# A decoder layer on one core: the eighth input of the first two feed-forward tiles last, and statistics ahead of the neighbour's finish

## The reference

```
h = silu(lin(x, w1)) * lin(x, w2)          # 256 -> 1024
h = gelu(lin(h, h1))                       # 1024 -> 1024
h = gelu(lin(h, h2))                       # 1024 -> 1024
y = lin(h, w3)                             # 1024 -> 256
x = layernorm(x + y)
```

## Time and profile before

| what | us |
|---|---|
| median of 3 runs | 927.42 |
| the profiled execution: its time | 932.09 |
| the profiled execution: its span in the trace | 930.3 |
| VectorE busy | 499.5 (54%) |
| ScalarE busy | 374.1 (40%) |
| GpSimd busy | 313.4 (34%) |
| mean granted clock of TensorE | 0.949 of full speed |

### The profile page before, as it was taken

The page is one execution under the profiler, slowest core; times in us unless marked ns, Lnnn a source line. Parts: engine busy times, 40 slices in busy tenths (PEclk is TensorE's granted clock), DMA queues, the critical chain, the costliest instruction groups (busy, mean ns, idle before and its releaser), DMA issues.

```text
span 930.3 us, 14113 instructions
## 1 busy us (share of the span) xinstructions
PE 865.7 (93%) x5066; PEld 572.7 (62%) x5066; DVE 499.5 (54%) x1299; ACT 374.1 (40%) x758; POOL 313.4 (34%) x553
## 2 busy tenths in 40 slices
PE   7779999898998999899999999999989999999996
PEld 5544444345766777786666644443467677887885
DVE  5597878625775432264444778873266752126113
ACT  0566666673444211232111366655635432123120
POOL 4403223136312544343132314213332143335333
PEclk9866989999999999999999889987799999999999
DMA  9800534240001233343231023520000000000000
GB/s 307 356 1 3 190 130 137 92 169 2 1 2 42 96 94 110 113 129 98 91 95 66 25 114 137 191 106 2 1 1 1 2 1 0 1 7 18 1 1 24
DMA packets 23894, 68.69 MB, mean 74 GB/s; under 512 B 4400, under 2 KB 11568, under 8 KB 23600
## 3 DMA queue, kind: packets, MB, share of 16 engines
q1 hardware_dynamic: 23824, 67.77, 20.8%
HBM read 65.40 MB, written 13.63 MB: 85 GB/s over the span
## 4 chain that ended last, share of the span: by engine, by line
PE 78%; DVE 13%; ACT 3%; issue 3%; POOL 2%; POOLq 0%; DVEq 0%; ACTq 0%
PE bank_pair L842 25%; PE bank_pair L667 7%; PE bank_pair L649 7%; PE bank_pair L618 7%; PE bank_pair L830 6%; DVE bank_pair L1165 4%; PE bank_pair L760 4%; DVE max_raw L1163 3%; PE bank_pair L699 3%; PE bank_pair L839 3%; PE bank_pair L604 3%; PE bank_pair L562 2%; PE bank_pair L772 2%; PE bank_pair L749 2%; PE bank_pair L716 1%
## 5 line engine op out<-in xcount | busy, mean ns | idle before, releaser
L986 ACT ACTIVATE prob_s<-bank_pair 128x512 f32<-128x512 f32 (+3 forms) x384 | 163.5, 495 | 86.7 <-PE bank_pair L649 85.8
L1455 POOL TENSOR_TENSOR hid_lo_s<-act_raw_s,hid_hi_s 128x512 fp32r<-128x512 f32 x96 | 124.3, 1295 | 216.8 <-DVE hid_hi_s L1321 176.5
L618 PE MATMUL bank_pair<-k_t_s,q_t_s 64*128 64x512 f32 (+3 forms) x384 | 149.2, 467 | 13.7 <-DVE max_raw L1165 7.6
L1165 DVE CUSTOM_DVE_ANT_0 bank_pair<-bank_pair,causal_bf 128x128 f32<-128x128 f32 (+3 forms) x256 | 123.4, 509 | 54.0 <-PE bank_pair L618 52.6
L1426 POOL TENSOR_SCALAR_AFFINE_SELECT prob_s<-prob_s 128x128 f32<-128x128 f32 x256 | 72.2, 297 | 170.0 <-ACT prob_s L986 166.8
L649 PE MATMUL bank_pair<-q_t_s,k_t_s 64*128 64x512 f32 (+3 forms) x384 | 119.0, 423 | 3.9 <-DVE resid_f_s L1285 1.7
L1321 DVE CAST hid_hi_s<-act_raw_s 128x512 fp32r<-128x512 f32 x64 | 31.7, 496 | 153.8 <-ACT act_raw_s L1047 153.8
L649 PEld LDWEIGHTS bank_pair<-q_t_s,k_t_s 64*128 64x128 f32 x384 | 60.3, 202 | 80.6 <-ACT prob_s L986 50.2
L618 PEld LDWEIGHTS bank_pair<-k_t_s,q_t_s 64*128 64x128 f32 x384 | 68.7, 207 | 62.9 <-issue 20.3
L1047 ACT ACTIVATE act_raw_s<-bank_pair,scales 128x512 f32<-128x512 f32 x64 | 43.7, 689 | 157.3 <-PE bank_pair L842 157.3
L1163 DVE TENSOR_REDUCE max_raw<-bank_pair 128x1 f32<-128x512 f32 x128 | 83.0, 685 | 43.1 <-PE bank_pair L618 43.1
(11 more groups left out here) (156 smaller groups left out, 1444.4 us busy)
## 6 DMA issues: line engine op xcount, KB each, us to landing
ring_s<-scratch SPq DMA_DIRECT2D x34, 512.0 KB, 3.3
home_s<-scratch SPq DMA_DIRECT2D x22, 512.0 KB, 5.9
checked_s<-in_w_ffn SPq DMA_DIRECT2D x2, 3584.0 KB, 17.8
scratch<-in_w_ffn SPq DMA_DIRECT2D x2, 2560.0 KB, 10.9
ring_moved_s<-scratch SPq DMA_DIRECT2D x10, 512.0 KB, 3.3
checked_s<-in_w_ffn SPq DMA_DIRECT2D x1, 4096.0 KB, 30.9
x_t_s<-in_x_t SPq DMA_DIRECT2D x2, 1024.0 KB, 5.2
x_tok_s<-in_x SPq DMA_DIRECT2D x2, 1024.0 KB, 8.7
```

The source lines that it names most:

```text
L618: mm(out[:, 0:k1 - k0], qkt(q, p, 0)[r, P * qt:P * (qt + 1)], qkt(q, p, 1)[r, k0:k1], start=True, stop=True).then_inc(S["max_mm"], 1)
L986: act.activation(prob[q][4 * (s % 2) + j][:, 0:n], S_BANK[j][:, 0:n], ACT.Exp, scale=SCALE).then_inc(S["exp_done"], 1)
L1165: dve.tensor_tensor_reduce(out=out[:, 0:left], in0=out[:, 0:left], in1=L["causal_bf"][:, CHUNK - left:CHUNK], scale=1.0, scalar=NEG, op0=A ...
L1455: pt(dst[1][:, m], act_raw[q][r % 3][:], dst[0][:, m].bitcast(F32), ALU.subtract).then_inc(S["f_lo"], 1)
```

## The change

The table of work is built by a new function. For h1, h2 and w3 the first two groups are written together: inputs 0 to 6 of tile 0, inputs 0 to 6 of tile 1, then input 7 of tile 0 and input 7 of tile 1. The groups from the third on are as before. On VectorE `out_finish` of a w3 tile is now issued behind `out_stats` of the next tile of its chunk, and that of the last tile (m = 3) one slot later at the end of `f_work`.

```diff
--- before.py
+++ after.py
@@ -214,13 +214,30 @@
     (1, 1, ("h2",), ("F", 1, 44), ("F", 1, 51)),
     (1, 1, ("w3",), ("F", 1, 52), ("F", 1, 55)),
 ]
+
+
+def products_in_order(groups):
+
+
+    last = KH - 1
+    work = []
+    for n, (layer, m) in groups:
+        if layer in ("w1", "w2"):
+            work += [(n, i) for i in range(4)]
+        elif m == 0:
+            work += [(n + j, i) for j in range(2) for i in range(2 * last)]
+            work += [(n + j, i) for j in range(2) for i in range(2 * last, 2 * KH)]
+        elif m >= 2:
+            work += [(n, i) for i in range(2 * KH)]
+    return work
+
+
 F_MM = [[] for _ in range(END_SLOT)]
 F_DONE = {}
 F_START = {}
 for _q, _c, _layers, _a, _b in PLAN:
     _a, _b = SLOT_AT[_a], SLOT_AT[_b]
-    _work = [(n, i) for n, (c, layer, m) in enumerate(GROUPS) if c == _c and layer in _layers
-             for i in range(4 if layer in ("w1", "w2") else 16)]
+    _work = products_in_order([(n, (layer, m)) for n, (c, layer, m) in enumerate(GROUPS) if c == _c and layer in _layers])
     for _j, (n, i) in enumerate(_work):
         _k = max(_a + _j * (_b - _a + 1) // len(_work), F_DONE.get((_q, n - len(F_BANKS)), -1) + 1)
         F_MM[_k].append((_q, n, i))
@@ -1299,9 +1316,6 @@
 
         def f_work(slot):
 
-            for q, n in F_FINISH[slot]:
-                c, layer, m = GROUPS[n]
-                out_finish(q, 4 * c + m)
             for q, n in F_AFTER[slot]:
                 c, layer, m = GROUPS[n]
                 if layer == "w2":
@@ -1320,8 +1334,15 @@
                     wait(dve, q, "f_act", r + 1)
                     dve.tensor_copy(hid[q][int(layer == "h1")][0][:, m], act_raw[q][r % 3][:]).then_inc(S["f_hi"], 1)
                 if layer == "w3":
+                    t = 4 * c + m
                     wait(dve, q, "f_mm", n + 1)
-                    out_stats(q, 4 * c + m, f_bank(n)[:, 0:D])
+                    out_stats(q, t, f_bank(n)[:, 0:D])
+                    if m:
+                        out_finish(q, t - 1)
+            for q, n in F_FINISH[slot]:
+                c, layer, m = GROUPS[n]
+                if m == 3:
+                    out_finish(q, 4 * c + m)
 
         def projections(q, t):
             if t < NT:
```

## The result

| what | before | changed |
|---|---|---|
| median on the same chip, 4 executions each | 927.48 us (925.76 to 927.61) | 914.38 us (913.79 to 915.99) |
| ratio, 95% interval | | 0.9862 [0.9836, 0.9888] |
| the profiled execution: its time | 932.09 | 913.79 |
| the profiled execution: its span | 930.3 | 912.0 |
| mean granted clock of TensorE | 0.949 | 0.965 |

The changed kernel is 13.1 us faster. The two profiled executions are 18.3 us apart, more than the medians, so part of that difference belongs to these two executions and not to the change. First the page, and the places of the sum.

The account below looks back on a forecast made before the run. TensorE, busy 865.7 of 930.3 us, was taken as the bound. Stops -1.3 and -1.2, VectorE -2.8 twice, clock -1.6 and self-attention +1.0 gave -8.7: 927.42 to 918.7 us, range 915.2 to 922.8.

Parts of the forecast that it names:

- A: w3 of sequence 0 chunk 0: TensorE's stop ahead of input 7 goes, 1.3 us; 2.9 us with the clock behind it.
- D: h1 of sequence 1 chunk 0: TensorE's stop ahead of input 7 goes, 1.2 us; 2.8 us with the clock.
- E: w3 of sequence 1 chunk 0: VectorE's chain of statistics and finishes ends 2.8 us earlier, and TensorE gains the same.
- the price of a dependent step: VectorE's multiplication waiting for the finish just ahead of it: 0.45 us, from 0.41 duration and a semaphore step.
- G: Last w3, at the program's end: the same VectorE chain as E, with only the store behind it, 2.8 us saved.
- the 5.7 of the prediction: Sign at G: the last finish comes under 4 us behind the last matmul, instead of 5.7.
- C: w3 of sequence 0 chunk 1, inside self-attention: the new order costs 0.8 to 1.2 us, taken as 1.0.
- The wait of the maximum unit and the 1.90 us: Signs at C: a new TensorE wait of about 1 us for a maximum, and 1.9 us ahead of the first score.
- The clock, 1.6 of 3.2: Behind the stops at A and D: TensorE's lower clock costs 3.2 us together; the middle, 1.6, was taken as regained.
- rival 3: Self-attention keeps the lower clock for longer: 933.7 us with 30 us more; chance 0.04 slower, 0.04 gain eaten to nothing.
- The prediction's own sign of being wrong: Between 530 and 680 us, granted clock differing by more than 10 us at half speed would show the prediction wrong.
- Nothing in the sum scales with that: The profiled execution's 4.7 us over the median was held not to affect the terms; 8.7 came off 927.42.

Follow-up runs that it names:

- p_before_12: Kernel before plus 12 idle transposes on TensorE ahead of sequence 1's projections; median 928.47 us, ratio 1.0024.
- best: Changed kernel with three tiles interleaved, inputs 6 and 7 last, at A and D, and the old product order at C; 917.49 us, ratio 0.9891.
- p_best_18: best plus 18 idle transposes on TensorE ahead of sequence 1's projections; median 914.89 us, ratio 0.9853.
- p_after_12: Changed kernel plus 12 idle transposes on TensorE ahead of sequence 1's projections; median 923.14 us, ratio 0.9937.
- e2_stats: Kernel before with only VectorE's new order (next tile's statistics ahead of the finish), products as before; median 921.39 us, ratio 0.9954.
- e6_h1_only: Kernel before with the new product order only in h1 of sequence 1 chunk 0; median 924.88 us, ratio 0.9967.

## Why the prediction was wrong in the time and right in the work

The part of the trace from A to the end of the span, which leaves out the 389 to 393 us whose code is the same in all kernels, and cut by its self-attention:

| | before | p_before_12 | changed | best | p_best_18 | p_after_12 |
|---|---|---|---|---|---|---|
| A to the end, us | 540.8 | 532.4 | 522.7 | 526.7 | 519.4 | 530.4 |
| of it score to D | 240.3 | 233.5 | 233.0 | 239.8 | 232.4 | 240.7 |

Between p_before_12 and the changed kernel, alike in self-attention, it is 9.7 us: 8.1 of work and the 1.6 of D's dip, where the forecast had 7.1 of work and 1.6 of clock. Between the two with the long self-attention, before and p_after_12, it is 10.4. The other 7 to 8 us, self-attention's, come and go on either side.

Term by term:

- **A, 1.3 of stop:** 12.59 (p_before_12, no dip) to 11.19 is 1.4. Right. The cover was there: no wait for input 7.
- **D, 1.2 of stop:** 60.33 to 59.15. Right.
- **E, 2.8:** 84.14 to 81.13, 3.0. Right, with the price of a dependent step 0.05 too low. The halves of the change are not additive there.
- **G, 2.8:** 14.52 to 11.84, 2.7. Right. From the end of TensorE's last matmul to the last finish it is 4.0 us (905.50 to 909.51), from 5.5 (922.31 to 927.77); the 5.7 of the prediction counts from that matmul's start.
- **C, a cost of 1.0:** the first score comes 0.7 later after w3's start, but of the stage behind it about 0.5 us come back (233.46 in p_before_12, 232.95 now). 0.2 us net. The wait of the maximum unit and the 1.90 us came as worked out; that VectorE's work brought forward no longer stands in the stage behind would explain the 0.5, and was left out of the sum; no run isolates it.
- **The clock, 1.6 of 3.2:** the step that failed, by its size and by its place. It measured 5.0 us in the first comparison (13.1 less 8.1 of work) and 4.1 in the pooled medians. Behind A and D the dips of 3.4 us are in no profile of a kernel with the new product order there, so all 3.2 of that came back where they had been. They are not in each execution of the kernel before either: p_before_12 has none at A, e2_stats none at D. But this term was sized for those two places alone, and rival 3 was held off with "the maxima and scores behind 541 us do not know of the feed-forward slots any more". They do not, but the granted clock over them changed all the same. The clock of that stage was treated as a part of the kernel before that stays when everything moves; it changed by 7.4 us in the profile, in the other direction than the rival had it. The prediction's own sign of being wrong came: from 530 to 680 us TensorE ran 39 us at 1.2 GHz before and 11 now, more than 10 us apart. "Nothing in the sum scales with that", said of the 4.7 us by which the profiled execution lay over the median, was the same step: that execution had 95 us at 1.2 GHz, where the executions of the kernel before have about 80 in the mean.

That the time fell outside the range at all is partly luck. The median of the first four executions lies 0.8 us below its low end, and the median of all 22, 915.2, lies on it. The mis-sized clock term, 4 to 5 us in place of 1.6, is in both.

What it is worth in the medians: the work terms give 1.4 + 1.2 + 3.0 + 2.7 - 0.2 = 8.1 us, and the pooled medians differ by 12.2. So 4 us are clock: the dips, self-attention, and the slow stretches ahead of A (last section) together. How they share it is not known, since only profiled executions show the places. A line through all executions, with a constant for each kernel, says 0.26 us of time per us at 1.2 GHz, and misses an execution by 0.85 us on average (root mean square). Mean time at 1.2 GHz is 78 to 85 us for the kernel before in its four comparisons with known clocks and 64, 75 and 73 us in the changed kernel's three. At equal time at 1.2 GHz the changed kernel is 8.2, 9.1 and 8.7 us faster, within 1 us of the work.

By the same account best is 10.2 us faster than before at equal clock, 1 to 2 more than the changed kernel, and lost it to the clock. p_best_18 (914.89, 0.9853 of its kernel before) stands level with the changed kernel; no version run here is clearly faster than it.

**What stays open:** why a shift of about a microsecond at the first score goes with slow stretches 100 us and more behind it, and how often an execution of each kernel has the long self-attention. No rule of the start time alone fits the 14 profiles; the order by the first slow stretch does for 11 of them, and for the three between it does not say which case comes.

## What to carry to other kernels

Two things were both true of this change: a sum of waits read from the timelines came within 1 us of the work saved (7.1 and 8.1), and the time missed the range because of the clock, above all in stages that nobody edited. Before a difference of a per cent is put down to an edit, look where the profiled execution lies among the other executions of its kernel, divide both traces at the same instructions, and look for a piece that changed with equal counts, equal busy time on the other engines and another granted clock. And where TensorE spends tens of microseconds at 1.2 GHz beside an edit, a blind forecast should carry that as a term of both signs; a pad of a microsecond of idle work tells afterwards how large it is.

## What the runs showed of the hardware that was not expected

- TensorE's clock in sequence 1's self-attention, a stage with hardly any long stop, can be 0.91 or 0.96 for the same instructions; 1.3 us of work more, 200 us earlier, went with 41 us at 1.2 GHz in place of 17 and a stage 7.5 us longer (240.7 and 233.1). The same code up to the end of the stage gave 240.3 us in the profile of the kernel before and 233.9 in that of e6_h1_only.
- What a microsecond at 1.2 GHz costs depends on the stage: 1.6 us for the 3.4 us at D (61.93 with, 60.33 without), 0.3 per us in self-attention (7.5 us for 24 us more), 0.26 over whole executions.
- The code ahead of A is the same in all kernels, but in the profiles it takes 389.3 to 393.1 us, a pad taken off. The short ones have one slow stretch at 128 us, the long ones two at about 168 to 171 and 191 us in its place. Between the same instructions the one at 128 costs 1.9 us, the one at 168 to 171 costs 1.2 (3.4 us long) or 3.1 (10.2 us long), and the one at 191 costs 1.5. That is as large as a term of the sum. Before and the changed kernel were short in each of their four profiles; since the code is the same everywhere, no edit of it is the cause, and what is stays open.
- Behind stops of 0.72 and 0.93 us, 1.6 us apart (D), a dip to 1.2 GHz stood in two profiles and was absent in a third; a single stop of 1.53 us (A in the changed kernel) had none in any.
